# Reloading the routed results after the scatters of the used tiles alone, from one queue

## The reference

```python
shared_enc = _expert_stack(x, sW1, sb1, sW2, sb2).sum(0)
weights = jax.nn.softmax(x @ gW + gb, axis=-1)
topv, topi = jax.lax.top_k(weights, TOP_K)              # 3 of 15 experts
gated = (jax.nn.one_hot(topi, E_ROUTER) * topv[..., None]).sum(axis=-2)
router_out = _expert_stack(x, rW1, rb1, rW2, rb2)       # 128 -> 256, gelu, -> 128
router_enc = jnp.einsum('ebtd,bte->btd', router_out, gated)
return shared_enc + router_enc + x                      # then a layer norm
```

## Time and profile before

| what | value |
|---|---|
| median of 3 runs | 347.08 us (346.86 to 347.74) |
| the profiled execution's own time | 346.81 us |
| its span | 345.0 us |
| PE busy | 255.0 us, 74% |
| DVE busy | 217.9 us, 63% |
| POOL busy | 212.8 us, 62% |
| ACT busy | 181.0 us, 52% |
| mean granted clock of PE | 0.862 of full speed |

### The profile page before, as it was taken

The page is one execution under the profiler, slowest core; times in us unless marked ns, Lnnn a source line. Parts: engine busy times, 40 slices in busy tenths (PEclk is TensorE's granted clock), DMA queues, the critical chain, the costliest instruction groups (busy, mean ns, idle before and its releaser), DMA issues.

```text
span 345.0 us, 7056 instructions
## 1 busy us (share of the span) xinstructions
PE 255.0 (74%) x2319; PEld 190.2 (55%) x2319; DVE 217.9 (63%) x578; ACT 181.0 (52%) x393; POOL 212.8 (62%) x219
## 2 busy tenths in 40 slices
PE   3989986776696877745997999879999898800700
PEld 1866755564452434314684867579998887700200
DVE  4568997974999999893646246446676555300650
ACT  2579792434769485423636242138886757700060
POOL 4426676425249994247788777617777777771480
PEclk9999999865999999875799579969999999965655
DMA  7974010124000077000111115233443333215512
GB/s 225 408 162 93 4 32 0 34 63 122 2 2 0 2 231 298 3 0 25 54 39 49 55 51 142 80 77 96 122 120 108 103 108 94 71 53 159 223 53 68
DMA packets 38196, 31.32 MB, mean 91 GB/s; under 512 B 12960, under 2 KB 31408, under 8 KB 37776
## 3 DMA queue, kind: packets, MB, share of 16 engines
q1 hardware_dynamic: 32448, 21.08, 21.0%
q0 software_dynamic: 3520, 7.27, 6.2%
q10 hardware_dynamic: 2192, 2.52, 2.4%
HBM read 19.38 MB, written 11.47 MB: 89 GB/s over the span
## 4 chain that ended last, share of the span: by engine, by line
POOL 33%; PE 23%; DVE 17%; issue 15%; DMA 7%; ACT 3%; SPq 0%; ACTq 0%; POOLq 0%; DVEq 0%
POOL x_srt L1558 13%; POOL k_heads L1527 6%; POOL v_pairs L1521 5%; PE psum L794 5%; PE psum L785 5%; POOL y_tok L1581 4%; DVE prob_sums L1227 3%; DMA y_tok<-k_heads,y_rows 2%; PE psum L582 2%; PE psum L481 2%; DMA v_pairs<-y_tok 2%; DVE maxes L1221 2%; DMA k_heads<-x_srt 1%; POOL rstd L1600 1%; DVE turned_room L1124 1%
## 5 line engine op out<-in xcount | busy, mean ns | idle before, releaser
L1581 POOL DMA_INDIRECT y_tok<-k_heads,y_rows x62 | 61.3, 989 | 27.6 <-issue 14.9
L1558 POOL DMA_INDIRECT x_srt<-v_blocks,slot x48 | 46.7, 974 | 14.3 <-issue 14.3
L1035 ACT ACTIVATE k_heads<-psum,k_heads 128x128 f32<-128x128 f32 x124 | 38.7, 365 | 16.9 <-PE psum L785 14.0
L1527 POOL TENSOR_TENSOR k_heads<-k_heads,inv_sums 128x1024 f32<-128x1024 f32 x16 | 30.9, 1934 | 26.9 <-DVE inv_sums L1232 26.9
L794 PE MATMUL psum<-k_heads 128*128 128x128 f32 x248 | 41.0, 289 | 4.4 <-ACT k_heads L1035 3.7
L785 PE MATMUL psum<-k_heads 128*128 128x128 f32 x248 | 39.9, 285 | 0.0
L794 PEld LDWEIGHTS psum<-k_heads 128*128 128x128 f32 x248 | 33.4, 196 | 8.0 <-ACT k_heads L1035 7.7
L785 PEld LDWEIGHTS psum<-k_heads 128*128 128x128 f32 x248 | 34.3, 200 | 0.5 <-DVE k_heads L1440 0.2
L1440 DVE COPY k_heads<-psum 128x128 f32<-128x128 f32 x62 | 18.0, 291 | 25.8 <-PE psum L777 25.2
L1424 DVE COPY k_heads<-expert_w 128x514 f32 x62 | 28.4, 464 | 3.4 <-issue 2.9
L1043 ACT ACTIVATE k_heads<-psum,k_heads 128x128 f32<-128x128 f32 x62 | 22.8, 368 | 13.9 <-DMA y_tok<-k_heads,y_rows 13.2
(11 more groups left out here) (161 smaller groups left out, 567.8 us busy)
## 6 DMA issues: line engine op xcount, KB each, us to landing
expert_w<-e_w SPq DMA_DIRECT2D x1, 4369.0 KB, 15.7
k_heads<-x_srt SPq DMA_DIRECT2D x62, 65.0 KB, 1.8
x_srt<-pad SPq DMA_DIRECT2D x16, 65.0 KB
xT<-x_t SPq DMA_DIRECT2D x4, 256.0 KB, 6.8
x_rows<-x_n SPq DMA_DIRECT2D x1, 1024.0 KB, 9.8
ctxT_k<-ctx_k SPq DMA_DIRECT2D x1, 1024.0 KB, 11.9
ctxT_v<-ctx_v SPq DMA_DIRECT2D x1, 1024.0 KB, 13.8
v_scr<-v_rows SPq DMA_DIRECT2D x4, 256.0 KB, 5.9
```

The costliest lines, as they stand in the source:

```text
L1035: ins = act.activation(h_tile[:, t % 2, a, :], bank[2 + t % 2][:, P * a:P * a + P], ACT.Gelu, bias=stage[:, t % NS, EW - 2 + a:EW - 1 + a])
L1527: pool.tensor_tensor(probs2[:, p % 3, :].rearrange("p (t h) -> p t h", t=B), probs2[:, p % 3, :].rearrange("p (t h) -> p t h", t=B), inv_s ...
L1558: pool.indirect_dma_start(out=x_srt, out_offset=bass.IndirectOffsetOnAxis(ap=slot[:, n:n + 1], axis=0), in_=payloads[:, g, k, :], in_offse ...
L1581: pool.indirect_dma_start(out=y_tok, out_offset=bass.IndirectOffsetOnAxis(ap=y_rows[:, t:t + 1].bitcast(mybir.dt.uint32), axis=0), in_=y_t ...
```

## The change

It adds a table `t_landed` of eight numbers: for each k from 0 to 7, 16 times the number of used tiles t with t mod 8 = k. Two DVE instructions make it from `tile_expert_f`, in the tile loop behind tile 8. After its last tile load SP loads the eight numbers to registers and waits for `s_y_scattered[k]` to reach them. SP then issues all twelve transfers of the reload, chunk by chunk, k = 0, 1, 2. ACT's waits and its part of the reload go. The results are reloaded to the rooms of `q_heads` (k = 0 and 1) and `ctxT_v` (k = 2), which nothing uses in the tile loop.

```diff
--- before.py
+++ after.py
@@ -150,6 +150,7 @@
         tile_row_f = sb("tile_row_f", [P, TABLE])
         t_expert = sb("t_expert", [1, TABLE], I32)
         t_row = sb("t_row", [1, TABLE], I32)
+        t_landed = sb("t_landed", [1, NB], I32)
         logit_max = sb("logit_max", [P, NG])
         logit_sum = sb("logit_sum", [P, NG])
         top_gates = sb("top_gates", [P, 4, 8])
@@ -188,9 +189,9 @@
 
         ctx_kv_room = k_heads2[:, :, :, :].rearrange("p a o m -> p (a o m)")
         v_pairs_room = v_pairs[:, :, :, :, :].rearrange("p g a b c -> p (g a b c)")
-        routed_y = [ctx_kv_room[:, 0:2048].rearrange("p (g e) -> p g e", e=E),
-                    ctx_kv_room[:, 2048:4096].rearrange("p (g e) -> p g e", e=E),
-                    v_pairs_room[:, 0:2048].rearrange("p (g e) -> p g e", e=E)]
+        routed_y = [q_heads_room[:, 0:2048].rearrange("p (g e) -> p g e", e=E),
+                    q_heads_room[:, 2048:4096].rearrange("p (g e) -> p g e", e=E),
+                    ctxT_v[:, :, :, :].rearrange("p o a b -> p (o a b)").rearrange("p (g e) -> p g e", e=E)]
         x2T = ctxT_k[:, :, :, :].rearrange("p o a b -> p (o a b)")
         gatesT = ctx_kv_room[0:NE + 1, 3072:4096].rearrange("p (a b) -> p a b", a=2)
         h_shared = xT[:, :].rearrange("p (a b c) -> p a b c", a=2, b=2)
@@ -257,6 +258,7 @@
         s_ends = sem("s_ends")
         s_filled = sem("s_filled")
         s_tables = sem("s_tables")
+        s_landed = sem("s_landed")
         s_x_tile = [sem(f"s_x_tile{k}") for k in range(NB)]
         s_tile_turned = sem("s_tile_turned")
         s_x_tileT = sem("s_x_tileT")
@@ -327,13 +329,12 @@
         CHAIN_BANK = (5, 5, 6, 7)
         GATE_BANK = (4, 5, 5, 5)
 
-        def reload_y(queue, half):
+        def reload_y(queue):
             for c in range(NC):
                 for k in range(TOPK):
-                    if (c + k) % 2 == half:
-                        queue.dma_start(routed_y[k][:, 4 * c:4 * c + 4, :],
-                                        y_tok[NT * P:NT * P + TOPK * T, :].rearrange("(k p g) e -> k p g e", g=NG, p=P)[k][:, 4 * c:4 * c + 4, :]
-                                        ).then_inc(s_y_loaded[c], 16)
+                    queue.dma_start(routed_y[k][:, 4 * c:4 * c + 4, :],
+                                    y_tok[NT * P:NT * P + TOPK * T, :].rearrange("(k p g) e -> k p g e", g=NG, p=P)[k][:, 4 * c:4 * c + 4, :]
+                                    ).then_inc(s_y_loaded[c], 16)
 
         def store(queue, c, ps):
             for j in ps:
@@ -410,9 +411,12 @@
                     sp.wait_ge(s_y_tile, t - NB + 1)
                     sp.wait_ge(s_y_rows, (t - NB) // 4 + 1)
                 sp.dma_start(x_tile[:, t % NB, :], x_srt[bass.ds(row_of[t % 4], P), :]).then_inc(s_x_tile[t % NB], 16)
+            sp.wait_ge(s_landed, 1)
+            landed = [sp.value_load(t_landed[0:1, k:k + 1], min_val=16 * (TOPK * T // P // NB), max_val=16 * (TABLE // NB))
+                      for k in range(NB)]
             for k in range(NB):
-                sp.wait_ge(s_y_scattered[k], 16 * ((NT + NB - 1 - k) // NB))
-            reload_y(sp, 0)
+                sp.wait_ge(s_y_scattered[k], landed[k])
+            reload_y(sp)
             for c in range(NC):
                 sp.wait_ge(s_final, c + 1)
                 if c == NC - 1:
@@ -1044,9 +1048,6 @@
                                    scale=x_tile[:, t % NB, E:E + 1]).then_inc(s_y_tile, 1)
 
 
-            for k in range(NB):
-                act.wait_ge(s_y_scattered[k], 16 * ((NT + NB - 1 - k) // NB))
-            reload_y(act, 1)
             for c in range(NC):
                 act.wait_ge(s_rstd3, 4 * c + 4)
                 for g in range(4 * c, 4 * c + (4 if c < NC - 1 else 2)):
@@ -1442,10 +1443,20 @@
             expert_of = None
             for t in range(NS):
                 expert_of = expert_staged(t, expert_of)
+
+            def tiles_landed():
+
+                routed(dve.tensor_scalar(tile_expert_f[0:1, :], tile_expert_f[0:1, :], float(NE), 16.0, ALU.is_lt, ALU.mult))
+                with nc.allow_low_precision(reason="whole numbers below 2**24"):
+                    dve.tensor_reduce(t_landed[0:1, :], tile_expert_f[0:1, :].rearrange("p (j k) -> p k j", k=NB), AX_X,
+                                      ALU.add).then_inc(s_landed, 1)
+
             for t in range(NT):
                 xinT_out(t)
                 if t % 4 == 1:
                     tile_rows(t - 1)
+                if t == NB:
+                    tiles_landed()
                 if NS <= t + 2 < NT:
                     expert_of = expert_staged(t + 2, expert_of)
```

## The result

| | kernel before | changed kernel |
|---|---|---|
| median | 347.23 us (346.86 to 347.74, 4 runs) | 336.68 us (336.1 to 337.4, 4 runs) |
| ratio to before | | 0.9696, 95% interval 0.967 to 0.9722 |
| profiled execution, its span | 346.81 us, 345.0 us | 337.11 us, 335.3 us |
| mean granted clock of PE | 0.862 | 0.867 |

The account below looks back on a forecast made before the run. POOL was taken to set the tile loop's pace, the last scatter's landing the reload's start. Reload at 302.95, plus 5.4 and 6.10, put the first rstd at 314.45, not 324.98: 346.81 - 10.5 = 336.3 us, range 334.4 to 339.0.

Parts of the forecast that it names:

- The wait: Before the reload, SP waits only for the 54 used tiles: waits end about 302.85 in place of 312.93, 10.1 us earlier.
- SP and the register loads: Eight register loads on SP after its last tile load: 2.4 us, at worst 6.2, hidden in 9.05 us, costed at nothing.
- The DVE instructions: Two counting instructions on DVE at tile 8, with waits some 0.5 us: costed at nothing, bounds 0 to 0.5.
- One queue: SP alone issues the reload at the old pace; c = 0 lands 5.4 us after its start, at 308.35; bounds 4.3 to 7.5.
- The empty scatters: POOL still issues the eight empty tiles' scatters beside the reload, unstretched, until 311.65; free at 313.3, before the first rstd.
- rival D: POOL's last eight scatters are held while the reload runs, so the kernel is slower: 352.0 us; chance 0.04.
- The sum: From landing of c = 0, 6.10 to first rstd at 314.45; shift 10.5, the 20.02 us behind it stay: 336.3 us.
- the gap: On SP, between the last awaited scatter's landing and the first reload issue: taken as 0.1 us, bounds 0 and 0.5.
- A: POOL's end becomes the bound before the first rstd: shift 11.4 to 12.0, about 335.2 us; chance 0.20.
- B: The reload starts slowly beside the scatters; c = 0 lands 7.5 after its start, shift 8.4: 338.4 us; chance 0.14.
- C: SP's wait isn't shortened, as tables count more tiles or SP arrives late: 1.26 per tile, 347 us; chance 0.04.

Follow-up runs that it names:

- e6_warm: Changed kernel plus six unread matrix products on PE between tile loop and reload; 384.11 us on a chip where the kernel before took 376.5 to 392.2.
- e7_warm_order: Changed kernel plus the six PE products, and DVE sums c = 0 before adding result 2 of c = 1; 384.04 us on the slow chip.
- f2_no_empty: Changed kernel with POOL leaving out the scatters of the eight empty tiles; 336.16 us, ratio 0.9668 to the kernel before.
- e3_constants: Changed kernel without the count: SP waits by constants for tiles 0 to 53, no DVE instructions or register loads; 336.92 us, ratio 0.9705.
- e4_58: As e3_constants, but SP waits for 58 tiles, four more than are used; 341.55 us, ratio 0.9823 to the kernel before.
- e1_all_waits: Changed kernel with SP waiting by constants for all 62 tiles' scatters, no count, single queue and new rooms kept; 346.19 us, ratio 0.9967.

## Why the prediction was right

**The wait.** It held. The used tiles are 54: the first issue follows the scatter that is the eighth before the last, and waiting for four more tiles moves the time by 4.1 to 4.6 us. The forecast had the first issue at 302.95; it was at 303.81. Of these 0.86, 0.76 are the tile loop's: the last scatter itself starts at 311.46 in this execution and at 310.70 in that of before, and over the runs with all 62 scatters that ran at the usual pace it starts between 310.46 and 312.36. That is no part of the change: the loop's first scatter is already 0.81 later (231.80 and 230.99), ahead of anything that was added.

**SP and the register loads.** At nothing, and right. The loads took 0.59 each in place of 0.3 to 0.77, 4.6 us in all, within 9 us of cover; 4.4 were left. The wait on registers, bounded by 0 and 0.5 and taken as 0.1, costs nothing against constants. The other 0.1 of the later issue is here: the gap after the landing is 0.21, which is what the earlier trace rows have, and I had taken 0.1.

**The DVE instructions.** 0.17 and 0.25 us, hidden.

**One queue.** c = 0 took 5.21 in place of the forecast 5.4; over the runs at the usual pace it took 4.69 to 5.68 with one queue, and 5.75 and 5.92 with two. For c = 1 the forecast had 311.1, 8.15 after the start; it was 8.24. For c = 2 it had 10.1, and it was 10.67 (PE at 314.48). That was just early enough: PE ended at 318.05 and DVE's sum of c = 2 began at 318.16.

By the estimate from the Trainium skill (DMA: Bandwidth & Descriptors, Anatomy of one DMA; a fixed 2.0 us and the bytes at 436 GB/s, there for GpSimd's path), c = 0 would have landed 3.8 after its issue. The runs at the usual pace have 4.69 at the least, so the measurement decides against it here. Two traces from the slow chip have less: in e6_warm DVE uses c = 0 3.47 after the first recorded issue, in e7_warm_order 4.64. But there the first two issues are recorded as 0.03 and 0.10 us long together, where the changed kernel's took 0.81, so I don't build on these starts. In e6_warm:

```profile
340.16 0.03 SPq L335 DMA_DIRECT2D q_heads<-y_tok  x2
...
343.63 0.69 DVE L1471 TENSOR_TENSOR x_rows<-x_rows,ctxT_v 128x512 f32<-128x512 f32 x1 [2.77 <-DMA ctxT_v<-y_tok]
```

In the changed kernel the windows show DMA busy and little moved at first (columns: from:to, length, busy of PE, PEld, DVE, ACT, POOL, then PEclk, DMA share, GB/s):

```profile
304.00:305.00 1.00, 0.00 (x0) 0.00 (x0) 0.00 (x0) 0.05 (x1) 0.85 (x1) 0.53 0.30 92
305.00:306.00 1.00, 0.00 (x0) 0.00 (x0) 0.00 (x0) 0.00 (x0) 0.85 (x1) 0.50 0.82 100
...
307.00:308.00 1.00, 0.00 (x0) 0.00 (x0) 0.00 (x0) 0.00 (x0) 0.69 (x2) 0.50 1.02 371
```

At 305 to 306 the DMA engines are busy 0.82 and move 100 GB/s, and 371 two microseconds later. PE's clock is at 0.50 (1.2 GHz) from 305 on, as the sum had it, and its addition took 3.75.

**The empty scatters.** POOL gave them out at 1.26 us each beside the reload, and rival D falls with that. It was free at 312.42, added c = 1, and stood 1.25 us; the forecast had 313.3 against 314.45, 1.15. That the bound is the landing and not POOL is shown by f2_no_empty, where POOL stood 9.90 us and the time from the first issue to the first rstd was 11.43, against 11.30.

**The sum.** The first rstd was forecast at 314.45 and came at 315.11: 0.86 for the later issue, less 0.19 for c = 0. The tail is 20.19 for 20.02. The forecast time stood against a profiled execution of 346.81; the changed kernel's profiled execution took 337.11, the longer for its later loop, and the medians moved by 10.55. Counted from the start of the last scatter, which takes the loop out, the first rstd moved from 14.28 to 3.65, by 10.63, and the mechanism accounts for the gain. That the medians agree with the forecast to 0.05 us is luck: the ratio's interval is 1.8 us wide, and the two terms that were off, the gap and c = 0, nearly cancel.

**The rivals.** A was closer than its 0.20 may suggest: POOL's end has 1.25 us to the bound, PE's half clock hides behind the landing of c = 1, and that of c = 3 is next. B (338.4) did not come; c = 0 was not over 5.92 in any run. C fell with e3_constants and e4_58.

## What to carry to other kernels

Where a program is laid out for the most work that there can be, a wait at its end for all of it can be cut to what was used, and the count may be read on the waiting queue as long as that queue has been idle; what it is worth is the pace of the engine that sets the loop, times the empty steps (here 8 x 1.26 us), as long as that wait is what comes last. The rooms that the early transfer writes must be free of the steps that still run. Behind such a wait read what comes next in the same trace: here the clock, the landings of the later parts and POOL's end lay within 1.3 us of each other, so removing one or two of them gave nothing that could be measured, and only the run that reordered three engines lies lower, by 1.6 us with intervals that still touch.

## What the runs showed that I had not expected

While the reload runs, POOL's scatters land late though they are given out on time. The transfers of the changed kernel from 296 us on (the last number is the median from issue to landing in us):

```profile
y_tok<-k_heads,y_rows POOLq DMA_INDIRECT x13, 4.8
```

The median is 4.8, where the last 13 scatters of the kernel before had 2.2; it is 2.2 again in e1_all_waits, where they all land before the reload starts. Eight of the 13 are the empty ones, for which nobody waits, so this costs nothing.
